# Three of 32 maximum tiles read by ScalarE instead of VectorE in the last attention of a gated cross-attention block

## What is computed

```python
qkv = (x @ W_qkv).reshape(Bx, Nx, 3, H, D)            # H = 16, D = 16
pos = sim > 0.9                                       # a class for each token
logits = jnp.einsum('bqhd,bkhd->bhqk', q * scale, k)
def masked_attn(tok_mask):
    key_mask = jnp.concatenate([jnp.ones((Bx, REG), bool), tok_mask], axis=1)
    l = jnp.where(key_mask[:, None, None, :], logits, -jnp.inf)
    a = jax.nn.softmax(l, axis=-1)
    return jnp.einsum('bhqk,bkhd->bqhd', a, v)
x_pos = masked_attn(pos)
x_neg = masked_attn(~pos)
tok_out = jnp.where(pos[:, :, None, None], x_pos[:, REG:], x_neg[:, REG:])
out = jnp.concatenate([reg_out, tok_out], axis=1).reshape(Bx, Nx, Cx)
return out @ W_proj + b_proj
```

## Time and profile before

| | |
|---|---|
| median of 3 runs | 1421.71 us (1420.78 to 1421.85) |
| the profiled execution | 1424.06 us, of which the recorded span is 1422.3 us |
| TensorE busy | 1264.7 us, 89% of the span |
| VectorE busy | 1044.8 us, 73% |
| ScalarE busy | 854.3 us, 60% |
| GpSimd busy | 160.5 us, 11% |
| mean granted TensorE clock | 0.942 of full speed |

### The profile page before, as it was taken

The page is one execution under the profiler, slowest core; times in us unless marked ns, Lnnn a source line. Parts: engine busy times, 40 slices in busy tenths (PEclk is TensorE's granted clock), DMA queues, the critical chain, the costliest instruction groups (busy, mean ns, idle before and its releaser), DMA issues.

```text
span 1422.3 us, 26541 instructions
## 1 busy us (share of the span) xinstructions
PE 1264.7 (89%) x10690; PEld 590.5 (42%) x10690; DVE 1044.8 (73%) x1563; ACT 854.3 (60%) x1432; POOL 160.5 (11%) x139
## 2 busy tenths in 40 slices
PE   4898974899899899948899999999999999999988
PEld 3566662454455755514433233232322333233237
DVE  4897494666664756545699999999999999999802
ACT  2233472666665155511287877887887787887871
POOL 2220021110600223310600000000000000000000
PEclk8977985999999999978799999999999999999999
DMA  5000026444450013340524443323443323443003
GB/s 177 24 1 14 1 29 111 95 85 89 90 90 2 0 67 133 134 94 11 82 50 69 82 79 57 75 54 64 82 81 62 67 56 63 82 81 48 2 1 118
DMA packets 78825, 92.56 MB, mean 65 GB/s; under 512 B 15210, under 2 KB 53356, under 8 KB 78704
## 3 DMA queue, kind: packets, MB, share of 16 engines
q1 hardware_dynamic: 78704, 90.87, 31.6%
HBM read 67.02 MB, written 23.80 MB: 64 GB/s over the span
## 4 chain that ended last, share of the span: by engine, by line
PE 58%; DVE 28%; ACT 7%; issue 4%; DMA 1%; SPq 1%; POOL 1%; DVEq 0%; ACTq 0%; POOLq 0%
DVE sm L1971 18%; PE ps L1460 9%; PE ps L1451 8%; PE ps L1432 6%; PE ps L1351 4%; ACT W L964 3%; PE ps L1216 2%; PE ps L1250 2%; PE ps L1570 2%; PE ps L1167 2%; PE ps L1358 2%; PE ps L1241 2%; PE ps L1299 1%; PE ps L1442 1%; PE ps L1387 1%
## 5 line engine op out<-in xcount | busy, mean ns | idle before, releaser
L1971 DVE TENSOR_REDUCE sm<-ps 128x1 f32<-128x1024 f32 x512 | 599.8, 1218 | 33.1 <-PE ps L1432 29.8
L964 ACT ACTIVATE W<-ps 128x512 f32<-128x512 f32 x1024 | 534.8, 604 | 140.2 <-PE ps L1460 136.3
L1460 PE MATMUL ps<-R 99*32 99x512 bf16 x4096 | 318.5, 383 | 6.2 <-ACT W L964 3.2
L1451 PE MATMUL ps<-W,R 128*32 128x512 f32 x2048 | 266.4, 596 | 0.7 <-ACT W L964 0.7
L1460 PEld LDWEIGHTS ps<-R 99*32 99x32 bf16 x4096 | 86.2, 94 | 225.4 <-ACT W L964 168.5
L882 ACT CAST R<-ps 4x2048 bf16<-4x2048 f32 x32 | 59.5, 1858 | 80.7 <-PE ps L1216 80.7
L1776 DVE TENSOR_REDUCE small<-ps 128x4 f32<-128x308 f32 x128 | 60.9, 477 | 62.6 <-PE ps L1205 62.2
L1432 PE MATMUL ps<-R 50*128 50x512 bf16 x512 | 89.2, 389 | 15.6 <-DVE sm L1971 12.9
L1432 PE MATMUL ps<-KM,R 50*128 50x512 bf16 x512 | 87.2, 384 | 9.6 <-DVE sm L1971 6.6
L1451 PEld LDWEIGHTS ps<-W,R 128*32 128x32 f32 x2048 | 63.2, 111 | 42.5 <-ACT W L964 1.4
L765 POOL COPY R<-R 128x512 f32<-128x512 f32 x16 | 10.3, 644 | 591.7 <-PE ps L1451 591.7
(11 more groups left out here) (258 smaller groups left out, 1587.1 us busy)
## 6 DMA issues: line engine op xcount, KB each, us to landing
R<-x_parts SPq DMA_DIRECT2D x96, 128.0 KB, 4.8
R<-q_parts SPq DMA_DIRECT2D x192, 64.0 KB
R<-q_parts SPq DMA_DIRECT2D x96, 128.0 KB
R<-k_parts SPq DMA_DIRECT2D x96, 128.0 KB
x_parts<-R SPq DMA_DIRECT2D x8, 768.0 KB, 4.1
q_parts<-R SPq DMA_DIRECT2D x24, 256.0 KB, 2.6
k_parts<-R SPq DMA_DIRECT2D x24, 256.0 KB, 2.6
X<-in_x SPq DMA_DIRECT2D x4, 1024.0 KB, 9.8
```

Source lines behind the costliest of these rows:

```text
L964: act.activation(PR[:, s % 2, h, :], third_bank("score", 64 * u + n), ACT.Exp, scale=0.25).then_inc(s_sfree, 1)
L1451: mm = pe.matmul(bank(7)[32 * h:32 * h + 32, :], VST[j][:, k, h, :], PR[:, s % 2, h, :], start=(k == 0), stop=(k == TB - 1))
L1460: mm = pe.matmul(o[32 * c:32 * c + 32, :], KST[j][0:MAX_ROW + 1, h, t:t + 32], QST[j][0:MAX_ROW + 1, h, 512 * (s // 8):512 * (s // 8) + 51 ...
L1971: dve.tensor_reduce(MX[:, half, h, q:q + 1], bank(2 * ((p + 1) % 2), 2), AX, ALU.max).then_inc(s_tfree, 1)
```

## The change

In the 15 full units three of the 32 tiles, a = 3, 7 and 11 (head 3, query blocks 0 to 2), are no longer reduced from PSUM by VectorE. ScalarE copies each as bf16 into an SBUF buffer `MT` (128 x 1024, the place of a weight that is no longer needed), placed behind the exponentials of slots 1, 3 and 5; this copy is what frees the pair of banks. VectorE folds the copy, 512 columns against 512, into one of three places of `MF`, ahead of the tiles of slots 2, 4 and 6. Behind the tiles of slots 6 and 7 it folds all three places together, 3 x 256 and then 3 x 128, and ahead of slot 8 one reduce of 3 x 128 gives the three columns of `MX`. The `rows` transpose of slot 9 now waits for that too. The rest of the program is as before.

```diff
+        COPIED = {3: 0, 7: 1, 11: 2}
+        GROUP = 6
...
+            def copy_tile(u, a):
+                p = PAIRS0 + 32 * u + a
+                act.wait_ge(s_turn, turn_of(u, a) + 1)
+                if copied_before(p):
+                    before = copied_before(p) - 1
+                    act.wait_ge(s_fold, GROUP * (before // 3) + before % 3 + 1)
+                act.copy(MT, bank(2 * ((p + 1) % 2), 2)).then_inc(s_tcp, 1)
+
             def body_act(u, last=False):
-                for s in ORDER:
+                for n, s in enumerate(ORDER):
...
+                    for a in (2 * n, 2 * n + 1):
+                        if a in COPIED and not last:
+                            copy_tile(u, a)
...
             def take_pair(p):
-                if p >= 2:
-                    pe.wait_ge(s_tfree, p - 1)
+                if p >= 2 and is_copied(p - 2):
+                    pe.wait_ge(s_tcp, copied_before(p - 1))
+                elif p >= 2:
+                    pe.wait_ge(s_tfree, p - 1 - copied_before(p - 1))
                 return bank(2 * ((p + 1) % 2), 2)
...
+            def fold_copied(g, i):
+                dve.wait_ge(s_tcp, 3 * g + i + 1)
+                dve.tensor_tensor(MF[:, i, :], MT[:, 0:512], MT[:, 512:1024], ALU.max).then_inc(s_fold, 1)
+
+            def fold_group(g, step):
+                n = (256, 128)[step]
+                dve.wait_ge(s_fold, GROUP * g + 3 + step)
+                dve.tensor_tensor(MF[:, :, 0:n], MF[:, :, 0:n], MF[:, :, n:2 * n], ALU.max).then_inc(s_fold, 1)
+
+            def reduce_group(g):
+                dve.wait_ge(s_fold, GROUP * g + 5)
+                dve.tensor_reduce(MX[:, 0, 3, 0:3], MF[:, :, 0:128], AX, ALU.max).then_inc(s_fold, 1)
...
             def body_dve(u, last=False):
                 n = PAIRS0 + TURNS * u
-                for what, arg in sum(PLAN_LAST if last else PLAN, []):
...
+                plan = PLAN_LAST if last else PLAN
+                for slot in range(len(plan) // 2 + 1):
+                    if not last and slot == 8:
+                        reduce_group(u)
+                    if not last and slot in (2, 4, 6):
+                        fold_copied(u, slot // 2 - 1)
+                    for what, arg in sum(plan[2 * slot:2 * slot + 2], []):
+                        if what == "tile" and arg not in COPIED:
+                            reduce_tile(n, PAIRS0 + 32 * u + arg, arg)
...
+                    if not last and slot in (6, 7):
+                        fold_group(u, slot % 2)
```

More of the change, by code:

```diff
@@ L310, in build_program @@
         Oe2 = XNf[:, 0:1024].rearrange("p (u n) -> p u n", u=2)
+        MT = wo1[:, :, :].rearrange("p j n -> p (j n)").bitcast(BF16)
+        MF = XNf[:, 1152:1920].bitcast(BF16).rearrange("p (k n) -> p k n", k=3)
         mro = XNf[0:16, 1024:1152].bitcast(BF16).rearrange("p (u n) -> p u n", u=2)
@@ L399, in build_program @@
         s_tfree = sem("pair_free")
+        s_tcp = sem("max_tile_copied")
+        s_fold = sem("max_tiles_folded")
         s_bfree = sem("small_turn_free")
@@ L456, in build_program, with copied_before, is_copied, turn_of @@
         TURNS = sum(len(x) for x in PLAN)
+        COPIED = {3: 0, 7: 1, 11: 2}
+        GROUP = 6
+        def copied_before(p):
+            p -= PAIRS0
+            return 0 if p <= 0 else len(COPIED) * (p // 32) + sum(a < p % 32 for a in COPIED)
+        def is_copied(p):
+            return p >= PAIRS0 and (p - PAIRS0) % 32 in COPIED
+        def turn_of(u, a):
+            return PAIRS0 + TURNS * u + sum(PLAN, []).index(("tile", a))
         SMALL = [("rows", 1), ("rows", 0), ("out", 0), ("out", 1)]
@@ L1474, in turns @@
                             o = take_third("small", small_turn(u, what, arg))
-                            pe.wait_ge(s_tfree, p + 16 * (1 - arg))
+                            ready = p + 16 * (1 - arg)
+                            pe.wait_ge(s_tfree, ready - copied_before(ready))
+                            if copied_before(ready):
+                                pe.wait_ge(s_fold, GROUP * (copied_before(ready) // 3))
                             max_rows(o, arg)
@@ L2007, in body_dve @@
                 n = PAIRS0 + TURNS * u
-                for what, arg in sum(PLAN_LAST if last else PLAN, []):
[L2009 to L2017, removed]
+                plan = PLAN_LAST if last else PLAN
[7 more added lines that the diff above has]
+                            reduce_tile(n, PAIRS0 + 32 * u + arg, arg)
+                        elif what == "rows":
+                            rows_turn(n, third_bank("small", small_turn(u, what, arg)), arg, s_bfree)
+                        elif what == "out":
+                            normalise2(n, third_bank("small", small_turn(u, what, arg)), u, arg)
+                        n += 1
+                    if not last and slot in (6, 7):
+                        fold_group(u, slot % 2)
             for u in range(UNITS):
```

## The result

The changed kernel takes 1441.24 us, the median of 4 runs (1438.33 to 1444.04); beside it on the same chip the kernel before took 1421.78 (1420.78 to 1422.66). The ratio is 1.0143, with a 95% interval of 1.012 to 1.0166: 19.5 us slower. The profiled execution took 1438.33 us, its span is 1436.6.

A forecast was written before the change was run, and what follows sets the result against it. It took a chain of waits between VectorE and TensorE, not one engine, as the bound. A unit 1.49 us longer, 15 times, adds 22.4 us to 1424.06; less 2.35 for the median, 1444 us, range 1432 to 1454.

The forecast's parts named there:

- Three waits go, one is worth something, and it moves: Slots 1 to 6: three reduces go, one 0.25 us wait goes, the other waits only change places.
- The copy delays a slot's fourth score product: Slots 2, 4, 6: copy holds the next exponential 0.88 us; product at S + 1.69, slot 0.17 us longer.
- Behind that, ScalarE has caught up.: After the late fourth product: a slot's four exponentials take 2.06 us, a slot 2.4 or more, so no further delay.
- The meeting with bank 7's copy: Slots 6 and 7: tile copy and bank 7's copy on ScalarE make them 5.56 us, listed as 0.63 us lost.
- Its list of parts: Per unit: 0.65 us group operations, 0.63 bank 7's copy, 0.5 three 0.17 delays, less the lost wait; total 1.49.
- The wait in slot 7: Sign: a wait of about 0.6 us for the fourth exponential should stand in slot 7's chain.
- The group operations: Slots 8 and 9: group folds and small reduce on VectorE make them 5.86 us, before 5.21; 0.65 us lost.
- The rival on the other side: Whole unit: VectorE is the bound, at most three pair waits (0.75 us) go, 1410.5 us; chance 0.07.

The follow-up runs named there:

- The relief alone: Kernel before with the reduces of tiles 3, 7 and 11 cut to 64 columns, nothing added: 1420.13 us, ratio 0.9998.
- The half tiles: Kernel before; for 14 of 32 tiles ScalarE copies 512 columns, VectorE reduces the other half; `rows` turns in slots 2 and 11: 1413.24 us, ratio 0.9961.
- the same order with whole tiles: Kernel before with only the two `rows` turns moved, to slots 2 and 11: 1423.55 us, ratio 1.0016.
- the first order: Kernel before, TensorE's tile 2n between third score product and values, `rows` and `out` turns ahead of odd tiles: 1454.2 us, ratio 1.0238.
- the second order: Kernel before, TensorE's tile 2n ahead of the third score product, `rows` and `out` turns ahead of odd tiles: 1433.22 us, ratio 1.008.

## Why the prediction was right

The forecast was 1444 us, the measurement 1441.24, with the same sign and by the mechanism given. Per unit it had 1.49 us, and the period shows 1.39; nearly all of the difference lies in one term, the group operations.

*Three waits go, one is worth something, and it moves.* Right to 0.02 us in every slot start up to slot 9. The relief alone would by this count be worth 0.25 us a unit; it gives nothing. The slot starts show that two free slots in a row do make the next one wait, and that the one wait that goes is given back in slot 7 by bank 7's copy. The prediction had reckoned with that copy for the full change only, and that the two amounts are alike (0.25 us) is a coincidence of this kernel.

*The copy delays a slot's fourth score product.* Right: 0.91 us to the next exponential (forecast 0.88), S + 1.67 (forecast 1.69). The product came no later for the 0.03 us, since the release of TensorE took 0.65 us (1015.40 to 1016.05) where I had 0.69. By the Trainium skill's rule of some 93 ns of overlap between activations ("ScalarE: Activation LUTs", What ACT_TABLE_LOAD costs) it would be 0.92, and the trace's 0.91 agrees with that better than with my own 0.88. By slot 6 the loss is 0.33 us (10.34 against 10.01), forecast 0.35.

*"Behind that, ScalarE has caught up."* This sentence was wrong, without harm. ScalarE is still 0.17 us late for the third score product of slots 3 and 5. The sum wasn't touched, because these slots wait for VectorE anyway; but the run with shortened reduces of tiles 4 and 8 shows that slots 3 and 5 are held by both engines, and that taking away VectorE's part gives back only 0.08 us of 0.25.

*The meeting with bank 7's copy.* Right: slots 6 and 7 take 5.58 us, forecast 5.56, before 5.07. The chain runs through ScalarE there as the prediction has it, and leaving out tile 11's copy gives 0.51 us back. The prediction called it 0.63 us against two free slots; against what stood there before, its own sum has 0.49 (5.56 - 5.07). Its list of parts therefore doesn't close: 0.65 + 0.63 + 3 x 0.17 - 0.25 is 1.54, and the missing 0.05 is the 0.06 us that slot 7 had lost before; the sum of the slots, which gave the forecast, has it right. The wait in slot 7 was to be about 0.6 us, and 0.48 us is what TensorE stood idle there.

*The group operations.* The mechanism was right, the size 0.11 us too large: slots 8 and 9 take 5.75 us, forecast 5.86, and without the group 0.54 us are gained, forecast 0.65. The durations were right (0.55, 0.35 and 0.553 us); the distances from start to start weren't. On VectorE the two reduces, the fold and the small reduce are followed after 2.27, 0.39 and 0.47 us (1030.20, 1032.47, 1032.86, 1033.33), where I had 2.36, 0.32 and 0.56, and tile 19 goes out 2.40 us later (1035.73), as I had it. That is 5.53 us, where I had 5.64 (15.82 to 21.46). The reduces and the small reduce are each followed 0.08 us ahead of their end, for which I had allowed nothing; the fold is followed 0.04 us behind its end, where I had its follower 0.03 us ahead of it.

The bf16 folds cost what the bf16 copy's rate said, not the fp32 rate of the earlier trace rows: 349, 426 and 550 ns for 384, 512 and 768 columns, 0.52 ns for each column over 0.15 us. The Trainium skill's table ("VectorE: DVE Perf Modes", the perf-mode tier table) has the two-input bf16 operation of 2048 columns at about half an fp32 one's time. The trace agrees in the rate, 0.52 against 1.06 ns for a column; at 512 columns the time itself is 0.62 of the fp32 one's (426 against 682 ns, the latter on 96 partitions).

*The rival on the other side* held VectorE to be the bound and gave 1410.5 us. Shortening three reduces refutes it for tiles 3, 7 and 11. It is half alive in another place. The rival gave the pair waits 0.75 us, three of 0.25 us. But over the whole unit of the kernel before the second tiles wait for 2.5 us: slots 0 and 11, the ones behind the `out` turns, lose 0.61 us each, and slot 13 loses 0.25, which the earlier trace rows doesn't cover. In slot 0:

```profile
1007.09 0.39 PE L1432 MATMUL ps<-R 50*128 50x512 bf16 x2 [0.44 <-DVE sm L1971]
```

The half tiles relieve 14 slots of 16, bring this down to 0.6 us, and gain 0.81 us a unit against the same order with whole tiles. So there was something to be had, but not from three tiles. Why ScalarE can bear the half copies better than the whole ones is not tested by itself, but the timelines show it in the fourth score product: behind a copy of 512 columns (0.64 us) it goes out at S + 1.52, as before, behind one of 1024 (1.01 us) at S + 1.67.

Two things stay open: why the same matmuls take TensorE longer when they stand apart, and whether the half tiles would gain more with the `rows` turns in a cheaper place, which wasn't tried.

## What to carry to other kernels

When two pairs of buffers are handed to and fro, relieving the consumer in single turns can merely move the wait to the next: ask what the turn after the relieved one does, and count the engine's slack in turns, not in busy time. Work given to an engine that looks idle (ScalarE, 60% of the span) is paid for at its next deadline; here it paid only in pieces that fitted into most turns, so keep the pieces short, and keep them away from the turns that already carry something extra. Small operations belong where their engine waits anyway: nine more of them there cost nothing, three elsewhere cost 0.54 us a unit.

## What the hardware showed that I had not expected

The time of a group of matmuls depends on what stands ahead of it, at full clock and with no wait in the chain: two maximum tiles take 0.54 us together and 0.32 each apart; twelve score matmuls 0.76 in one piece and 0.55 + 0.33 in two; the eight fp32 records of the values 0.86 behind score matmuls and 0.99 behind a maximum tile. That turned two expected gains into losses, of 0.8% where no wait was left and of 2.4% where 1.1 us of waits per unit stayed as well. It isn't a fixed price for each change of kind: the first order has one change more in a slot than the kernel before and the second has two, and their slots are 0.24 and 0.22 us longer. The ends of matmuls are modelled in such records, but the period of the second order, which GpSimd shows, bears its sum out (43.2 us).
